# Local attention: the mask written into the score banks by ACT instead of by products on PE

## The reference, cut to what matters

```
bk2, bv2 = (look(bk), look(bv))            # a window's keys: the window before it, and its own
mask = (it < jb) | (it > jb + w) | (jb == -1)
sim = einsum('bhwie,bhwje->bhwij', bq, bk2) * QK_SCALE
sim = where(mask, -finfo.max, sim)
attn = softmax(sim, -1)
out = einsum('bhwij,bhwje->bhwie', attn, bv2)
```

## Time and profile before

| | |
|---|---|
| Median of 3 runs | 4250.97 us (4242.65 to 4258.53) |
| Span of the profiled execution, the only time that the page gives for it | 4257.0 us |
| PE busy | 3863.2 us (91% of the span) |
| DVE, ACT, POOL busy | 2486.2, 1981.1, 1636.8 us |
| Projections L1707 on PE, 2304 passes | 1065.6 us |
| Mask products L1744 on PE, 768 | 78.7 us |
| `exp` L1851 on ACT, 192 | 203.6 us |

### The profile page before, as it was taken

The page is one execution under the profiler, slowest core; times in us unless marked ns, Lnnn a source line. Parts: engine busy times, 40 slices in busy tenths (PEclk is TensorE's granted clock), DMA queues, the critical chain, the costliest instruction groups (busy, mean ns, idle before and its releaser), DMA issues. The chain is left out here.

```text
span 4257.0 us, 68864 instructions
## 1 busy us (share of the span) xinstructions
PE 3863.2 (91%) x26887; PEld 2079.8 (49%) x26887; DVE 2486.2 (58%) x3451; ACT 1981.1 (47%) x3526; POOL 1636.8 (38%) x1428
## 2 busy tenths in 40 slices
PE   6769976889999999999999999999999999998755
PEld 4433433545544555445544555445554455545423
DVE  4564555578823886258842788238862588424533
ACT  3455543556632664336632566326643366323412
POOL 0520321066611664136630566117641366300035
PEclk9989987999999999999999999999999999998877
DMA  4000000121110111011120111101110111100396
GB/s 148 1 23 21 0 1 11 45 56 29 27 62 17 29 29 52 26 25 29 29 68 0 35 29 27 61 17 29 29 55 23 25 29 30 47 0 11 102 280 187
DMA packets 95680, 185.74 MB, mean 44 GB/s; under 512 B 14088, under 2 KB 46592, under 8 KB 94336
## 3 DMA queue, kind: packets, MB, share of 16 engines
q1 hardware_dynamic: 87152, 169.28, 13.6%
q0 software_dynamic: 6144, 9.44, 1.2%
q10 hardware_dynamic: 2064, 2.62, 0.2%
HBM read 112.45 MB, written 20.09 MB: 31 GB/s over the span
## 5 line engine op out<-in xcount | busy, mean ns | idle before, releaser
L1707 PE MATMUL PS<-locw,X 128*128 128x512 f32 x2304 | 1065.6, 599 | 32.1 <-PEq L133 13.1
L1977 POOL TENSOR_TENSOR locm<-locm 128x512 f32<-128x512 f32 x384 | 489.2, 1274 | 891.1 <-DVE locm L1913 890.6
L1707 PEld LDWEIGHTS PS<-locw,X 128*128 128x128 f32 x2304 | 394.9, 190 | 444.0 <-issue 312.9
L2096 PE MATMUL PS<-locxn,locw 128*128 128x512 f32 x960 | 429.6, 605 | 20.0 <-DVE loch L2220 20.0
L1983 POOL TENSOR_TENSOR locm<-locm,locrn 128x512 f32<-128x512 f32 x384 | 392.2, 1042 | 129.3 <-ACT locrn L1826 129.3
L1990 POOL TENSOR_TENSOR locpr<-locpr,locrs 128x512 f32<-128x512 f32 x384 | 391.0, 1039 | 128.8 <-DVE locrs L1942 109.0
L1929 DVE TENSOR_REDUCE locnm<-PS 128x8 f32<-128x1024 f32 x192 | 235.1, 1225 | 269.9 <-PE PS L1749 269.9
L1847 ACT ACTIVATE locpt<-PS 128x512 f32<-128x512 f32 x384 | 208.7, 596 | 326.3 <-PE PS L1717 326.3
L2220 DVE SCALAR_TENSOR_TENSOR loch<-PS,locvec,locgl 128x512 f32<-128x512 f32 x144 | 106.7, 748 | 356.4 <-PE PS L2096 266.7
L1816 ACT ACTIVATE locsq<-PS 128x512 f32<-128x512 f32 x384 | 229.9, 599 | 179.2 <-PE PS L1707 179.2
L2096 PEld LDWEIGHTS PS<-locxn,locw 128*128 128x128 f32 x960 | 183.8, 194 | 263.1 <-issue 233.1
(11 more groups left out here) (330 smaller groups left out, 6399.5 us busy)
## 6 DMA issues: line engine op xcount, KB each, us to landing
locve<-locva SPq DMA_DIRECT2D x372, 128.0 KB, 2.2
locw<-in_L2f_wqkv SPq DMA_DIRECT2D x36, 512.0 KB, 9.4
BIG<-in_L3f_gu SPq DMA_DIRECT2D x16, 768.0 KB, 9.5
moe_sums<-none SPq DMA_DIRECT2D x2, 4352.0 KB, 24.0
locw<-in_L2f_w SPq DMA_DIRECT2D x6, 1386.0 KB
BIG<-moe_sums SPq DMA_DIRECT2D x16, 512.0 KB, 9.5
moewp<-in_L3f_gu SPq DMA_DIRECT2D x10, 768.0 KB, 13.3
loctab<-in_L2f_tabs SPq DMA_DIRECT2D x6, 1024.0 KB, 12.1
```

Of the source, the lines that this page charges most:

```text
L1707: mm = pe.matmul(PS[:, o % 2, :], k.X[:, j, at - j:at - j + P], W[:, j, col:col + G], start=j == 0, stop=j == KD - 1)
L1977: pool.tensor_tensor(M1[:, j, :], M1[:, j, :], M2[:, x, :], ALU.add).then_inc(s.paired, 1)
L2096: mm = pe.matmul(PS[:, 4 + 2 * (m % 2) + half, :], W1[:, c, at:at + P], XNL[:, g % 2, c, :], start=c == 0, stop=c == KD - 1)
```

## The change

For each half ACT writes the mask into banks 4 and 5 (`mask(u)`, one ACTIVATE Copy of 128x1024 from bf16 in SBUF to PSUM, the 512 columns of the table read twice). It stands in ACT's queue behind `exp(u)` and ahead of `out(u-1)`, writes for half u+1, and waits for `shifted(u)`; `mask(0)` stands at the head of the layer. The score products add onto what ACT has written, and `scores_may_start` waits for `masked` in the place of `shifted`. The four mask products of a half are gone. At the head of each layer PE writes the two banks with a 128x512 product each, on which `mask(0)` waits. In the mask table, kind 0 now masks the window before only for the first 64 rows, since one instruction writes both windows.

```diff
-    mask = np.stack([np.tile(np.concatenate([v, own], 1), (1, 4)) for v in (none, before)], 1).astype(f)
+    first = np.where(np.arange(P)[:, None] < WIN, none, before)
+    mask = np.stack([np.tile(np.concatenate([v, own], 1), (1, 4)) for v in (first, before)], 1).astype(f)
...
                         def scores_may_start(u):
 
                             def gate():
-                                if u:
-                                    pe.wait_ge(s.shifted, HALVES * layer + u)
-                                else:
+                                pe.wait_ge(s.masked, HALVES * layer + u + 1)
+                                if u == 0:
                                     pe.wait_ge(s.cleared, 2 * layer + 2)
                                 pe.wait_ge(s.turned, ready_turn(u, 1) + 1)
                             return gate
 
                         def scores(u):
                             n, i = divmod(u, 2)
-                            for r in range(2):
-                                for w in range(2):
-                                    kind = 0 if n % NT == 0 and w == 0 else 1
-                                    pe.matmul(PS[w * WIN:(w + 1) * WIN, 4 + r, :], k.identb[r * HD:(r + 1) * HD, r * HD:(r + 1) * HD],
-                                              MASKB[r * HD:(r + 1) * HD, kind, :], start=True, stop=False)
                             for t in range(4):
                                 for r in range(2):
                                     for w in range(2):
                                         mm = pe.matmul(PS[w * WIN:(w + 1) * WIN, 4 + r, t * P:(t + 1) * P],
                                                        QT[r * HD:(r + 1) * HD, 4 * i + t, w * WIN:(w + 1) * WIN],
                                                        KT[n % 2][r * HD:(r + 1) * HD, 4 * i + t, w * WIN:w * WIN + P],
-                                                       start=False, stop=t == 3)
+                                                       start=False, stop=t == 3, skip_group_check=True)
                             mm.then_inc(s.scores, 1)
...
+                        for r in range(2):
+                            mm = pe.matmul(PS[:, 4 + r, :], k.identb[:, :], MASKB[:, 0, :], start=True, stop=True)
+                        mm.then_inc(s.primed, 1)
                         pe.wait_ge(s.weights, 96 * layer + 96)
...
+                        def mask(u):
+                            if u:
+                                act.wait_ge(s.shifted, HALVES * layer + u)
+                            else:
+                                act.wait_ge(s.primed, layer + 1)
+                            kind = 0 if u // 2 % NT == 0 else 1
+                            act.activation(PS[:, 4:6, :], MASKB[:, kind, :].unsqueeze(1).to_broadcast([P, 2, G]), ACT.Copy).then_inc(s.masked, 1)
+
                         nc.scalar.preload_act_table_set(LNEXP)
+                        mask(0)
...
                             exp(u)
+                            if u < HALVES - 1:
+                                mask(u + 1)
                             if u:
                                 out(u - 1)
```

More of the change, by code:

```diff
@@ L1573, in stage_local_transformer @@
         s.wo_in_psum, s.x1, s.gate_in_psum, s.a_in_psum, s.gelu, s.h, s.y_in_psum, s.x2, s.mean_in_psum, s.xsum, s.centred, s.fsquared, s.sqsum,
-        s.var_in_psum, s.log_var, s.rstd, s.xnormed, s.affine, s.rest
+        s.var_in_psum, s.log_var, s.rstd, s.xnormed, s.affine, s.rest, s.primed, s.masked
     ) = (sem("loc_" + n) for n in (
@@ L1580, in stage_local_transformer @@
         "wo_in_psum", "x1", "gate_in_psum", "a_in_psum", "gelu", "h", "y_in_psum", "x2", "mean_in_psum", "xsum", "centred", "fsquared", "sqsum",
-        "var_in_psum", "log_var", "rstd", "xnormed", "affine", "rest"
+        "var_in_psum", "log_var", "rstd", "xnormed", "affine", "rest", "primed", "masked"
     ))
```

## The result

The changed kernel takes 4320.45 us (median of four runs, 4313.39 to 4326.94) against 4250.71 before: 1.0153 times as long, with a 95% interval of 1.0134 to 1.0173. A second series gave 4329.42 against 4257.66: 1.0177 (1.0161 to 1.0192). The change makes the kernel slower by 1.5 to 1.8%.

A forecast was written before the change was run, and what follows sets the result against it. The prediction took PE's work and a loop through ACT, PE and DVE to bind equally at 9.55 us a half; -46 + 94 + 3 = +51 us gave 4308 profiled, 4302 expected, range 4268 to 4362.

The forecast's parts named there:

- What bounds the kernel: Attention halves: PE's own work and a loop through ACT, PE and DVE, both taken to set the 9.55 us period.
- both bind at once: Attention half: the loop through ACT, PE and DVE sums to 9.55 us, claimed just as long as PE's own work.
- the ring: Loop from one `exp` through ACT, PE and DVE to the next: 9.55 us, forecast to become 9.85.
- Part 2: ACT's mask write between `exp` and `out`: delays the queries copy by 0.54 us, costing 174 x 0.54 = 94 us.
- m: Time from the start of ACT's mask write to the next instruction's start: taken as 0.95 us, ends 0.48 and 1.24.
- Part 1: PE's mask products removed ahead of the scores: gain 0.24 us a half, 46 us in all; lower bound 25 us.
- Part 3: Layer heads: PE's two bank-writing products cost 3 us in all; ACT's first mask fits before the first square.
- The sum: Whole kernel: -46 + 94 + 3 = +51 us, giving 4308 for the profiled execution and 4302 expected, 1.2% slower.
- The hidden mask: Rival: ACT's write fits free time between `exp` and the queries copy, needing under 0.66 us; 4220 us, chance 0.06.
- The slow write to two banks: Rival: ACT's mask write to PSUM takes 1.24 us, a delay of 0.83; 4352 us, chance 0.09.
- The clock rival: Rival: PE's gaps in attention halves drop the granted clock to 0.91, adding 52 us; 4354 us, chance 0.05.
- The only-seeming wait: Rival: later values would not hold up PE's second projection, so the write costs nothing there; 4208 us, chance 0.02.

The follow-up runs named there:

- run 2: Changed kernel with ACT's mask write moved behind the values copy and PE's wait for it moved directly ahead of the first score: 4234.27 us, 0.9944 of before.
- run 4: Kernel before without its four mask products a half and nothing in their place, so scores are unmasked: 4224.78 us, 0.9926 of before.
- run 6: Changed kernel with ACT's mask write one place later, behind `out` instead of ahead of it: 4373.51 us, 1.0279 of before.
- run 3: Kernel before plus an ACT copy of the same size into an unused SBUF tile, between `exp` and `out`: 4345.39 us, 1.0211 of before.
- run 5: Changed kernel with ACT writing the mask into bank 5 only and PE making bank 4's two mask products: 4272.30 us, 1.0030 of before.
- runs 1: Changed kernel with only ACT's mask write moved, behind the values copy and ahead of the square: 4244.65 us, 0.9970 of before.
- run 7: The changed kernel measured again, nothing altered: 4329.42 us, 1.0177 of before.

## Why the prediction was right, and what was off

**What bounds the kernel** was right in the step that decided. PE was busy for 100% of the stretch, and yet work on ACT that PE's second projection comes to wait for is not free. With the mask products gone, the same write costs nothing in run 2 (a period of 9.37, as in run 4 without any mask), 0.51 us a half in the changed kernel (9.88) and 0.85 in run 6 (10.22), by its place alone.

The reason that the prediction gave for it, "both bind at once", does not follow from its sum. Steps that are read from one start to the next, once round a half, add up to the period whatever binds it. The 1.85 us from `exp` to the queries held time in which ACT waits for PE; in a queue without a gap they are 0.97 + 0.47 = 1.44. So the ring itself was 9.14 us long, with 0.41 of room, and did not bind before the change. The forecast took no harm, because Part 2 takes this 0.41 off m. The runs measure the room, as the length of what was put in less what the period grew by: 0.95 - 0.52 (run 3), 0.52 - 0.09 (run 5) and 0.95 - 0.51 (the changed kernel against run 4), so 0.43 to 0.44. Of the 0.02 to 0.03 above 0.41, most lies in the copies behind the write: from the queries to the values it is 1.24 us before and 1.22 after, in the mean of the steady halves. In the same way the room behind `out` is 0.10 (0.95 - 0.85, run 6), and behind the values at least the 0.95 that the write takes (run 2).

PE's idle time, forecast as 0.54 a half, is 0.29 in the bracket and 0.45 by the starts of the passes: there as forecast, but not to be sized by the bracket.

**Part 1** had the mis-sized term. The products are worth 0.18 a half and not 0.24 (run 4), so 35 us in all and not 46. I had argued from the transposes, whose first product begins with its first load, and had taken the scores and their loads as unchanged. They are not. Before, the loads for the scores began under the mask products, at 1507.83, 0.21 us ahead of the first score (1508.04); in run 4 they begin together with the first score, at 1524.94, and the row of scores takes 1.10 us instead of the 1.04 of the earlier trace rows. Before (the first row) and run 4 (the second):

```profile
1507.83 1.01 PEld L1749 LDWEIGHTS PS<-lockt,locqt 64*64 64x64 f32 x32
```

```profile
1524.94 0.86 PEld L1744 LDWEIGHTS PS<-lockt,locqt 64*64 64x64 f32 x32 [0.76 <-issue]
```

The lower bound of 25 us held.

**Part 2** was right in its mechanism and its size. The mask row's median is 1.01 us, and from start to start it takes the 0.95 that was taken:

```profile
L1873 ACT ACTIVATE PS<-locmaskb x192: 1008/1010/1028, 868.3 to 3716.4; 128x1024 f32<-128x1024 bf16 x192
```

The delay came out at 2.39 - 1.85 = 0.54, as forecast. The Trainium skill (Perfetto Trace Analysis, Optimizing Scalar/DVE Operations) states a lower fixed cost of ScalarE on PSUM than on SBUF. In the same place the copy into SBUF of run 3 took 1.05 us (median) and the write to PSUM 1.01, so the row agrees; but from start to start both took 0.95, and the 7 us that the rule would have given were not there. Behind the values (runs 1 and 2) the write's row is 1.06 us long, and it is 0.95 from start to start there too.

**Part 3** held: ACT's first mask of a layer fits between the table load and the first square. The square starts 1.10 us behind the end of the table load instead of 0.75, so 0.35 a layer or 2 us in all are lost, where 3 were forecast. Timeline of ACT at a layer's start, beside the earlier trace rows:

```profile
1375.22 1.28 ACT L1875 ACT_TABLE_LOAD   x1 [20.48 <-PEq L2041]
...
1376.51 1.03 ACT L1873 ACTIVATE PS<-locmaskb 128x1024 f32<-128x1024 bf16 x1
...
1377.60 0.60 ACT L1814 ACTIVATE locsq<-PS 128x512 f32<-128x512 f32 x1
```

**The sum** was +51; with the measured terms it is 174 x (0.54 - 0.03) = 89, less 192 x 0.18 = 35, and 2 at the layers' starts: +56, the 0.03 being what the room had above 0.41. The profiled executions differ by 54.6. The medians differ by 70, and by 72 in the second series. The remaining 15 us were in no step of the prediction; that the time still lies in the range is owed to the range's width, made for an uncertain m. In the trace of run 7 they lie in the passages between layers, at the lower clock. Of the runs without a trace the time and the mean clock are on record: a common straight line through 30 runs of the kernel before and the nine of the changed one leaves 62 us between them at an equal mean clock (an estimate). By it the clock brings about half of what the medians have above +56, and the other half stays open.

**The rivals.** The hidden mask (4220 us) fell: its condition was m below 0.66. It was right that ACT has room for the write, in another place: run 2 put it there and gained 0.6%. The slow write to two banks fell (0.95, not 1.24). The clock rival fell in its place: with PE idle for a part of every half, the attention phase stayed at 1.00. In another place, the passages, the clock did bring the 15 us of run 7's trace that were not forecast. The only-seeming wait fell: PE's weight loads now wait 90 us longer in all for the values.

## What to carry to other kernels

An engine that is busy all the time need not leave the others free. Before work is moved to a second engine, follow the loop from engine to engine and take out of each step the time in which an engine only waits for another. What is then missing to the period is the room of that place; with the waits left in, the steps always add up to the period and say nothing. What is put in beyond the room is paid in every round, however idle the engine is in the mean: here the same 0.95 us met a room of 0.43 ahead of `out`, 0.10 behind it, and at least 0.95 behind the values. So the place of an instruction in an in-order queue can matter more than its length. Put new work behind the instruction that another engine waits for, and make the consumer wait only where it needs the data.

## What the runs showed of the hardware

- ACT's 128x1024 write from bf16 to two PSUM banks takes 1.01 us beside PE's work on other banks (1.06 in runs 1 and 2), and 0.95 from start to start, as much as a copy to SBUF (run 3).
- Here a product that was taken away returned less than its own time, since the loads of the next products had run under it: four products that held the scores up by 0.24 us were worth 0.18 (run 4).
- The attention period repeats to a hundredth of a microsecond in every layer of a trace, and in both traces of the changed kernel, but the time of a whole run varies by some 0.6% with the share at the lower clock elsewhere. In 18 runs of the kernel before, the mean granted clock goes from 0.954 (4275.51 us, the slowest) to 0.961 (4248.09, the fastest). The changed kernel has 0.954 to 0.960 over nine runs, the kernels of runs 1 and 2 0.953 to 0.958. The passages between layers take 193 to 198 us, by their granted clock. A change of some microseconds in the length of a layer may shift where the stretches at the lower clock fall, and so move the median by some microseconds that no stage accounts for; that is not shown. Why they fall differently from one run to the next stays open; nothing here was made to test it.
